# Linear-attention stage: the orders of all engines rearranged, state and turned input made early, the softplus correction subtracted ahead of the logarithm

## The reference

```python
qkv = in_proj_weight * x + in_proj_bias          # 3 parts of A = 4 features per token
q, k = softplus(q), softplus(k)
s = cumsum(k_i * v_j);  z = cumsum(k)            # along the tokens
y = sum_i(q_i * s_ij) / sum_i(q_i * z_i)         # then moved on by one token, first = 1
y = sum_j(hid_w[a, :, j] * y_j) + hid_b[a]       # for a = 0..3
out = sum_a(out_w[a] * tanh(y_a)) + out_b
```

## Time and profile before

| what | value |
|---|---|
| median of 3 runs | 3336.93 us (3336.86 to 3338.26) |
| profiled execution, its own time | 3336.11 us |
| its span | 3334.3 us |
| mean granted TensorE clock, of full speed | 0.699 |
| PE, DVE, ACT, POOL busy | 48%, 59%, 24%, 54% |

### The profile page before, as it was taken

The page is one execution under the profiler, slowest core; times in us unless marked ns, Lnnn a source line. Parts: engine busy times, 40 slices in busy tenths (PEclk is TensorE's granted clock), DMA queues, the critical chain, the costliest instruction groups (busy, mean ns, idle before and its releaser), DMA issues. The chain is left out here.

```text
span 3334.3 us, 31491 instructions
## 1 busy us (share of the span) xinstructions
PE 1608.9 (48%) x11604; PEld 935.7 (28%) x11604; DVE 1976.1 (59%) x1764; ACT 798.1 (24%) x1078; POOL 1815.2 (54%) x1353
## 2 busy tenths in 40 slices
PE   4666442222232222232222201627887888878887
PEld 3454310000010000010001001514454554455455
DVE  4222245555555555554555554757888888887885
ACT  2111241111111111111111101533433333433431
POOL 2000037777777777777777773345544554455442
PEclk8788765555555555555555555868989899989999
DMA  9999764555555555545555533121212221122112
GB/s 370 406 429 429 316 163 119 144 155 153 137 135 136 138 149 149 137 136 138 136 149 146 137 114 137 27 89 61 66 60 72 100 67 60 60 94 85 60 57 86
DMA packets 337892, 483.65 MB, mean 145 GB/s; under 512 B 186016, under 2 KB 277940, under 8 KB 320048
## 3 DMA queue, kind: packets, MB, share of 16 engines
q1 hardware_dynamic: 279120, 330.24, 29.6%
q0 software_dynamic: 58720, 152.72, 16.1%
HBM read 397.28 MB, written 85.45 MB: 145 GB/s over the span
## 5 line engine op out<-in xcount | busy, mean ns | idle before, releaser
L440 POOL DMA_INDIRECT gath<-table,idx x1152 | 1207.1, 1048 | 439.6 <-issue 378.4
L615 DVE TENSOR_TENSOR gath<-gath,p_stat 128x2304 f32<-128x2304 f32 x128 | 326.9, 2554 | 747.4 <-DMA gath<-table,idx 708.9
L652 PE MATMUL p_z<-wz,pairs 128*128 128x384 f32 x384 | 264.2, 820 | 458.5 <-issue 454.1
L498 ACT ACTIVATE zt<-p_z 128x384 f32<-128x384 f32 x192 | 93.5, 491 | 982.2 <-remote 526.1
L1268 PE MATMUL p_state<-xt,tri 128*128 128x512 f32 x512 | 258.9, 653 | 62.7 <-DVE prod L1156 62.7
L1036 POOL TENSOR_TENSOR query<-query,expo 128x2048 f32<-128x2048 f32 x16 | 102.1, 6379 | 334.5 <-DVE query L1134 334.5
L652 PEld LDWEIGHTS p_z<-wz,pairs 128*128 128x128 f32 x384 | 100.3, 300 | 611.1 <-issue 599.1
L1156 DVE TENSOR_TENSOR prod<-p_state,query 128x2048 f32<-128x2048 f32 x80 | 183.0, 2288 | 128.3 <-PE p_state L1273 128.3
L642 PE MATMUL p_conv<-sides,wconv 128*128 128x512 f32 x64 | 66.3, 1140 | 398.1 <-issue 331.4
L1304 PE MATMUL p_sum<-ident,prod 128*128 128x128 f32 x1024 | 173.5, 341 | 105.5 <-DVE prod L1178 105.5
L1178 DVE TENSOR_TENSOR prod<-hidw,y 128x2048 f32<-128x2048 f32 x64 | 208.8, 3283 | 6.1 <-DMA hidw<-in_hidw 4.4
(11 more groups left out here) (230 smaller groups left out, 3106.0 us busy)
## 6 DMA issues: line engine op xcount, KB each, us to landing
ring<-in_w SPq DMA_DIRECT2D x64, 2304.0 KB, 19.4
hidw<-in_hidw SPq DMA_DIRECT2D x64, 1024.0 KB, 5.0
table<-zt SPq DMA_DIRECT2D x256, 144.0 KB
table<-zt SPq DMA_DIRECT2D x512, 72.0 KB
gath<-table,idx POOLq DMA_INDIRECT x1152
xt<-in_x SPq DMA_DIRECT2D x4, 1024.0 KB, 8.1
resid<-xt SPq DMA_DIRECT2D x32, 128.0 KB, 2.4
xlate<-resid SPq DMA_DIRECT2D x16, 256.0 KB, 2.9
```

The lines of the kernel that those rows point to most:

```text
L440: nc.gpsimd.indirect_dma_start(out=gath[:, t % SLOTS, k].rearrange("p n c -> p (n c)"), out_offset=None, in_=tables[u], in_offset=bass.Ind ...
L615: tt(g, g, w, ALU.mult).then_inc(weighted, 1)
L652: nc.tensor.matmul(p_z[i % ZS][:], pairs[u][:, 4 * J:4 * J + 4].rearrange("p j w -> p (j w)"), wz[:, m * WIDE:(m + 1) * WIDE], start=True, ...
```

## The change

The per-stage semaphores of the group norms become one set that all four stages share, so that their waits count on (turn 1 to 6) over the stages. The rest is in `layer3`:

- Softplus: ACT also does Relu (after the Copy, in place on key or query). POOL's subtraction `take_lost` then waits for Relu and the correction, and no longer for the logarithm; DVE's `add_log` adds the logarithm afterwards with a plain addition, and waits for both. The expo tile is free once POOL has subtracted (`eased`), lift once DVE has added (`soft`).
- PE: state 0 of batch b + 1 comes ahead of the first hidden sum of batch b, the turn of batch b + 2 ahead of its third. The output of batch b - 1 stands after state 4. `hidden` is split in `hidden_bias` and `hidden_sum`.
- DVE: TQ0 (`times_query` 0) heads the batch; key and value are projected after it and the query after the second; the key's correction moves from ahead of the third product to after the first division; the key's addition moves from ahead of the fourth to after the second division; the scan of the column sums moves ahead of the hidden products, the query's addition between the second and third of them.
- POOL adds the key's bias before the value's.
- ACT does the softplus of key and query first, then take_out, then the normalisation. take_out(b - 1) now waits for the divisions of batch b, since o and recip share a tile. The out_done semaphore starts at 16, so that the reciprocal of batch b waits for the store issued in the batch before.

```diff
-            def softplus_end(part, b, g):
-                pool.wait_ge(relud, b * 2 + (g + 1))
-                tt(part[:], part[:], expo[:], ALU.subtract).then_inc(soft, 1)
+            def take_lost(part, b, g):
+                pool.wait_ge(rectified, b * 2 + (g + 1))
+                pool.wait_ge(lost_ready, b * 2 + (g + 1))
+                tt(part[:], part[:], expo[:], ALU.subtract).then_inc(eased, 1)
             def inputs(b, u):
+                add_bias(key, 1, k_scaled, b, biased)
                 add_bias(value, 2, v_scaled, b, v_ready)
-                add_bias(key, 1, k_scaled, b, biased)
                 add_bias(query[u], 0, q_scaled, b, biased)
-                softplus_end(key, b, 0)
-                softplus_end(query[u], b, 1)
+                take_lost(key, b, 0)
+                take_lost(query[u], b, 1)
...
             def exponential(part, b, g):
                 act.wait_ge(biased, b * 2 + (g + 1))
                 if not (known(b) and b == 0 and g == 0):
-                    act.wait_ge(soft, b * 2 + g)
+                    act.wait_ge(eased, b * 2 + g)
                 nc.scalar.activation(expo[:], part[:], ACT.Abs).then_inc(absd, 1)
                 act.wait_ge(absd, b * 2 + (g + 1))
                 nc.scalar.activation(expo[:], expo[:], ACT.Exp, scale=-1.0).then_inc(expd, 1)
                 act.wait_ge(expd, b * 2 + (g + 1))
+                if not (known(b) and b == 0 and g == 0):
+                    act.wait_ge(soft, b * 2 + g)
                 nc.scalar.activation(lift[:], expo[:], ACT.Copy, bias=1.0).then_inc(lifted, 1)
+                nc.scalar.activation(part[:], part[:], ACT.Relu).then_inc(rectified, 1)
...
             def main(b, u, left):                       # ACT
-                if not (known(b) and b == 0):
-                    take_out(b - 1)
                 if left:
                     exponential(key, b + 1, 0)
                     logarithm(b + 1, 0)
+                    exponential(query[1 - u], b + 1, 1)
+                    logarithm(b + 1, 1)
+                if not (known(b) and b == 0):
+                    take_out(b - 1, b + 1)
                 if left == 2:
                     normalise(b + 2)
-                if left:
-                    exponential(query[1 - u], b + 1, 1)
-                    logarithm(b + 1, 1)
...
-            def relu_log(part, b, g):
+            def add_log(part, b, g):
                 dve.wait_ge(logd, b * 2 + (g + 1))
-                stt(out=part[:], in0=part[:], scalar=0.0, in1=lift[:], op0=ALU.max, op1=ALU.add).then_inc(relud, 1)
+                dve.wait_ge(eased, b * 2 + (g + 1))
+                tt(part[:], part[:], lift[:], ALU.add).then_inc(soft, 1)
...
             def main(b, u, left):                       # DVE
+                times_query(b, u, 0)
                 if left:
                     dve.wait_ge(x_turned, b + 2)
+                    project(key, 1, k_scaled)
                     project(value, 2, v_scaled)
-                times_query(b, u, 0)
+                times_query(b, u, 1)
                 if left:
-                    project(key, 1, k_scaled)
                     project(query[1 - u], 0, q_scaled)
-                times_query(b, u, 1)
                 denominator(b, u)
-                if left:
-                    lost_part(b + 1, 0)
                 times_query(b, u, 2)
                 divide(b, u, 0)
                 if left:
-                    relu_log(key, b + 1, 0)
+                    lost_part(b + 1, 0)
                 times_query(b, u, 3)
                 divide(b, u, 1)
                 if left:
+                    add_log(key, b + 1, 0)
                     keys_x_values(b + 1, 0)
                     keys_x_values(b + 1, 1)
                 times_query(b, u, 4)
...
+                if left:
+                    column_carries(b + 1)
                 hidden(b, u, 0)
-                if left:
-                    relu_log(query[1 - u], b + 1, 1)
                 hidden(b, u, 1)
                 if left:
-                    column_carries(b + 1)
+                    add_log(query[1 - u], b + 1, 1)
                 hidden(b, u, 2)
                 hidden(b, u, 3)
...
             def main(b, u, left):                       # PE
-                if left:
-                    turn(b + 1)
-                state(b, 0)
+                state(b, 1)
+                sum_terms(b, u, 0)
+                state(b, 2)
+                sum_terms(b, u, 1)
+                state(b, 3)
+                sum_terms(b, u, 2)
+                state(b, 4)
                 if not (known(b) and b == 0):
                     output(b - 1)
-                for n in range(1, TERMS):
-                    state(b, n)
-                    sum_terms(b, u, n - 1)
-                sum_terms(b, u, A)
+                sum_terms(b, u, 3)
+                sum_terms(b, u, 4)
                 if left:
                     totals(b + 1, (A, 0, 1, 2, 3)).then_inc(totalled, 1)
-                for a in range(A):
-                    hidden(b, u, a)
+                hidden_bias(b, u, 0)
+                if left:
+                    state(b + 1, 0)
+                hidden_sum(b, u, 0)
+                hidden_bias(b, u, 1)
+                hidden_sum(b, u, 1)
+                hidden_bias(b, u, 2)
+                if left == 2:
+                    turn(b + 2)
+                hidden_sum(b, u, 2)
+                hidden_bias(b, u, 3)
+                hidden_sum(b, u, 3)
```

More of the change, by code:

```diff
@@ L31, in __call__, with group_norm_vector @@
         self.eng.wait_ge(self.sem, self.n)
-def group_norm_vector(nc, dve, link, x, t, s, row_stats=None):
+def group_norm_vector(nc, dve, link, x, t, s, row_stats=None, turn=1):
     if row_stats is None:
@@ L45, in group_norm_vector @@
     last.then_inc(s["row_stats"], 1)
-    join_groups_vector(nc, dve, link, t["mv"][:, :, 0], t["mv"][:, :, 1], B, t, s)
+    join_groups_vector(nc, dve, link, t["mv"][:, :, 0], t["mv"][:, :, 1], B, t, s, turn)
     link(nc.vector.scalar_tensor_tensor(out=t["shift"][:, 0:B], in0=t["mean"][:, 0:B], scalar=-1.0,
@@ L86, in stat_buffers, with layer0 @@
     t["ps"] = ctx.enter_context(nc.psum_tensor(f"{tag}_ps", [P, 2 * B], F32)) if ps is None else ps
[L87 to L92, removed]
+    return t
+def layer0(nc, xt, d, row_stats, tables, gs):
     NQ, PX = 4, 8
@@ L904, in early_tiles, with layer3 @@
     return tiles, ctx.enter_context(nc.semaphore("early_in"))
-def layer3(nc, xt, d, out, early, row_stats, resid, saved):
+def layer3(nc, xt, d, out, early, row_stats, resid, saved, gs):
     A = ATT
@@ L1220, in _ @@
             dve.wait_ge(x_turned, 1)
+            project(key, 1, k_scaled)
             project(value, 2, v_scaled)
-            project(key, 1, k_scaled)
             project(query[0], 0, q_scaled)
             lost_part(0, 0)
-            relu_log(key, 0, 0)
+            add_log(key, 0, 0)
             for j in range(A):
                 keys_x_values(0, j)
+            column_carries(0)
             lost_part(0, 1)
-            relu_log(query[0], 0, 1)
-            column_carries(0)
+            add_log(query[0], 0, 1)
             over_batches(dve, main)
@@ L1290, in sum_terms, with hidden_bias @@
                 last.then_inc(summed, 1)
-            def hidden(b, u, a):
+            def hidden_bias(b, u, a):
                 r = (u + TERMS + a) % 2
@@ L1300, in hidden, with hidden_sum @@
                                      start=(k == 0), stop=False, is_transpose=True)
+            def hidden_sum(b, u, a):
+                r = (u + TERMS + a) % 2
                 pe.wait_ge(hid_scaled, b * A + (a + 1))
@@ L1322, in main @@
             def main(b, u, left):
-                if left:
-                    turn(b + 1)
-                state(b, 0)
+                state(b, 1)
[5 more added lines that the diff above has]
+                state(b, 4)
                 if not (known(b) and b == 0):
                     output(b - 1)
-                for n in range(1, TERMS):
-                    state(b, n)
-                    sum_terms(b, u, n - 1)
-                sum_terms(b, u, A)
+                sum_terms(b, u, 3)
+                sum_terms(b, u, 4)
                 if left:
                     totals(b + 1, (A, 0, 1, 2, 3)).then_inc(totalled, 1)
-                for a in range(A):
-                    hidden(b, u, a)
+                hidden_bias(b, u, 0)
[10 more added lines that the diff above has]
+                hidden_sum(b, u, 3)
             turn(0)
             totals(0, (A, 0, 1, 2, 3)).then_inc(totalled, 1)
+            state(0, 0)
+            turn(1)
             over_batches(pe, main)
@@ L1343, in build_program @@
 def build_program(nc, d, out):
-    with nc.sbuf_tensor("xt", [P, B, HALF], F32) as xt, nc.sbuf_tensor("row_stats", [P, B, 6], F32) as row_stats:
+    with nc.sbuf_tensor("xt", [P, B, HALF], F32) as xt, nc.sbuf_tensor("row_stats", [P, B, 6], F32) as row_stats, ExitStack() as whole:
```

(9 more changed lines are left out.)

56 lines of the change are left out of this document (28 added, 28 removed).

## The result

The changed kernel takes 3215.26 us (median of 4 runs, 3212.62 to 3217.28) against 3337.6 before (median of 4): ratio 0.9634, 95% interval 0.9622 to 0.9647.

The account below looks back on a forecast made before the run. DVE and PE, both busy 82% of the middle stretch, wait for each other. From 3336.11 us, less 124.9 (batches of 59.5) and 8.5 (prologue), plus 2.0 (tail), comes 3204.7; with 0.8 for the median 3205.5, range 3180 to 3245.

Parts of the forecast that it names:

- Early state and turn: Head of the batch: state 0 and turn move among the hidden products, so waits of 3.1 and 2.4 us go.
- Key's bias first, correction late, TQ3's wait of 1.5: POOL and DVE, early batch: the late key's correction takes turns (0.5 us), then TQ3 waits 1.5 for state 3.
- Subtraction ahead of the logarithm: POOL subtracts for the key before DVE adds the logarithm; the added wait holds DVE 0.2 us.
- The first hidden product waits 1.8 for its turn: DVE beside POOL's second subtraction (40.4 to 44.9 us): first hidden product waits 1.8 and ends at 47.1.
- Weights: Third hidden product: 0.8 us idle for weights, then turns of 0.4 and 1.25 with POOL's gated products.
- Relu covered: ACT: Relu adds 3.8 us a batch, the key's has 3.5 of cover before the subtraction; cost taken as nothing.
- Output behind state 4: PE: the output's sum (3.15 us) moves behind state 4, with cover of 4.6; tail +2.
- The clock: PE's slow pieces: 59.5 us a batch taken, between 58.4 at 2.4 GHz and 60.0; ends 58.4 and 61.5.
- Rival (a): Slow pieces fall on states 1 and 3, and 0.7 is missing: 62.2 us a batch, 3246; chance 0.13.
- (c): Slower than before: TensorE at 1.2 GHz in the states, 69.3 us a batch, 3352; chance 0.02.
- (b): Thinner cover: weights land after 8 us, Relu on the path in half its cases: 62.9 a batch, 3257; chance 0.08.
- (d): Fewer turns between DVE and POOL: with none 54.9 us a batch, 3136; half of them 3171; chance 0.07.

Follow-up runs that it names:

- e_state_late: Changed kernel with state 0 and the turn back at the head of PE's batch: 3342.23 us, ratio 1.0016 to the kernel before.
- e_old_softplus: Changed kernel with the softplus of the kernel before (no Relu on ACT, POOL's subtraction after the logarithm): 3292.98 us, ratio 0.9867 to the kernel before.
- e1_scan_first: Changed kernel with the scan of the column sums ahead of the edge operation on DVE: 3203.18 us, ratio 0.9600 to the kernel before.
- e_weights_once: Changed kernel without reloading hidden weights (first two sets used throughout, so another output): ratio 0.9616 to the kernel before on the same chip.
- e_query_dve: Changed kernel with the query's subtraction on DVE, fused with the maximum, no Relu for the query: ratio 0.9576 to the kernel before on the same chip.
- v_both: Changed kernel with the query's subtraction on DVE and POOL's gated products after the fourth hidden product: ratio 0.9556 to the kernel before on the same chip.
- v_three: Changed kernel, POOL's gated products late, query's subtraction on DVE just ahead of the query's add_log: ratio 0.9544 to the kernel before on the same chip.
- e_relu_twice: Changed kernel with Relu done twice on ACT for key and query: ratio 0.9618 to the kernel before on the same chip.

## Why the prediction was right, and where its sizes were off

1. *Early state and turn.* Right. TQ0 follows the last hidden product at once in 11 of 15 batches, and e_state_late shows it worth 125 us of the middle stretch, more than the two old stalls of 5.5 us a batch together, since the new DVE order leaves nothing to do there.
2. *Key's bias first, correction late, TQ3's wait of 1.5.* Measured 1.7, and 0.4 of turns for the correction (2.68 for 2.28) where the sum had 0.5: the fused operation does take turns, as the Trainium skill (SBUF — State Buffer, "SBUF: two separate sides") has it.
3. *Subtraction ahead of the logarithm.* The wait it adds is 0.2 as worked out. That without it the batch would be 4.9 longer was not priced in the prediction; e_old_softplus shows it.
4. *The first hidden product waits 1.8 for its turn.* This is the step that failed. The first hidden product takes its plain 2.27; the sign "first hidden product at 4.1" did not come. The edge correction stands ahead of it and takes the turn itself: 3.47 - 0.29 = 3.2 a batch, with the scan behind it instead of beside it. I had counted turns for two SBUF tiles only, and this operation reads one, with two scalars from the edge tile. The term was 1.4 a batch too small, 21 us in 15 (e1_scan_first gives 13.6 of them back). The Trainium skill (SBUF — State Buffer, "Who interferes with whom") says that a tensor_scalar can enter a mode that uses two ports, and can then contend with GpSimd when its operands meet the mode's conditions. The trace agrees that it contends, 3473 ns against 294 in the kernel before; whether the mode or the two scalars make it so, no run here tells.
5. *Weights.* 0.8 of waiting forecast, 1.1 measured. The layout had 5.1 us from release to landing for both loads, where the earlier trace rows had 6.5 for the second. Turns with the gated products: 1.7 forecast, 0.9 measured. The two errors partly cancel, since with the weights there the products meet POOL in full (e_weights_once).
6. *Relu covered.* Right, with room for a second one. The price of 57 us that the prediction worked out for the rule on relu of the Trainium skill (ScalarE: Activation LUTs, "Rules for kernel authors") did not show. Whether a Relu on DVE would have been as cheap here is not shown: with the maximum fused into DVE's addition the subtraction has to wait for the logarithm, and that batch is 4.9 longer (e_old_softplus); fused into a subtraction on DVE it came with the gain of e_query_dve.
7. *Output behind state 4.* No wait of a division on PE in the middle stretch, as forecast. The tail is 3.0 longer, forecast 2: 2.3 between TQ4 and the last division, where the output is, and 0.9 at the very end, where PE's third hidden sum is slow in this run (3.49 for 1.97). The prologue gained 7.6 of the 8.5 forecast, lost in steps of 0.1 to 0.3 each.
8. *The clock.* Forecast 1.1 us a batch for slow pieces, ends 0 and 3.1. That a state would be slow in each batch was wrong: all but one of the 60 take 3.60 or 3.70. The one is in batch 0 (6.59 after a rest of 7.69), and it makes half of the 5.8 us by which the 15 intervals exceed 15 times 59.8. One hidden sum is still slow in most batches (3.06 to 3.60 for 1.97), but DVE hardly waits for it: 2.5 us in all. The granted clock is 0.97, and the matmuls of the states average 611 ns against 656. So the clock cost at most 0.4 a batch, 10 us less than forecast.

In sum, the 60.2 a batch hold 3.9 of waits (3.1 in the layout) and 4.5 of turns (4.0). The edge term was 21 us too small and the clock term 10 us too large, and the middle stretch came out 10 us over the forecast: that the time is no further off is in part luck. Rival (a) needed two slow states in each batch, (c) all of them slow: neither came. Of (b) neither part came: the weights landed 4.8 to 6.7 us after release and not 8, and Relu cost nothing. (d), fewer turns, didn't come either.

The layouts made ahead of the runs gave 58.7 a batch for e1_scan_first (measured 58.7 to 59.1 in most), 58.7 for e_query_dve (58.7 or 58.8 in 8 of 15), 57.6 for v_both and 59.2 afterwards, with the two loads 3.8 apart (58.2 to 59.1 in most), 57.1 for v_three (57.5 to 59.1), 67.3 for e_state_late (68.5) and 64.1 for e_old_softplus (65.1). Where they are off by more than half a microsecond, slow pieces on PE or the spacing of the loads account for it in part; in e_old_softplus that was not followed up.

Left open: what decides in which batch PE's hidden sum falls slow in v_three was not tried. The orders on DVE, POOL and ACT were not taken apart, and the early state was not tried in the old DVE order, so the 125 us belong to it only with the rest in place. Nor is it told apart how much of the 108 us between the chips is the gathers and how much PE: in the gather stage PE's 384 matmuls of 128x384 average 570 ns on the one chip (e_relu_twice) and 814 on the other (changed).

## What to carry to other kernels

Lay out one period with every engine's queue from the durations of the old trace before moving anything; here it gave the batch to within 2% (59.5 for 60.2), with two errors that partly cancelled. Measuring the parts alone would have misled: the split gains nothing without the early state, and the new orders, early state included, give 45 of 122 us without the split. Count turns between DVE and POOL for every DVE operation that reads SBUF only, the tiny ones too: the 32x4 one here waited out what was left of a POOL instruction of 4.5 us. A wait in the trace is worth its length only if nothing stands ready to take its place. The second of two loads released 2.2 us apart landed 5.4 to 6.7 us after its release, where one released 4.4 behind the other mostly took 5, so give it more cover.

## What the runs showed of the hardware

- A DVE operation on 32x4 elements with one SBUF tile as input and two scalars from SBUF, 294 ns alone, took 3473 ns beside a POOL subtraction of 4535 and ended with it; operations that read one PSUM and one SBUF tile were not held up beside POOL (2.29 us for the fourth product with the query in the changed kernel, 1.22 for the scan in e1_scan_first).
- Loads of 1 MB from one queue, from the release of the buffer to the landing: released 4.4 us apart, as in the kernel before, most of them landed within 4.8 to 5.3 us. Released 2.2 apart, as in the changed kernel, the first landed after 4.8 to 6.2 and the second after 5.4 to 6.7, 2.5 to 3.9 apart. The earlier trace rows show one such pair: 4.9 and 6.5, 3.8 apart.
- One chip ran the stages before this one in some 108 us less than the others, for all four kernels profiled there, while the last stage took the same (903.2 for e_relu_twice there, 902.8 for the changed kernel here).
